# Self attention on one core: token-wise softmax sums folded into the output gates, masked rows on the scalar engine, joins on the vector engine

## The chip, the cores and the metric

The kernel runs on one core of a Trainium2 chip. The engines that matter here are TensorE (PE, with its weight loads listed apart as PEld), VectorE (DVE), ScalarE (ACT) and GpSimd (POOL); each works through its own instructions in program order and waits on semaphores for the others. The metric is the device time of one execution in microseconds (us), as the median of repeated runs.

## The reference, cut to what matters

The program is four layers over x of shape (4, 512, 256): two cross attentions, a routed feed-forward layer, and at the end a self attention with expert gates. The change touches the last one alone:

```python
B, T, D = (4, 512, 256)
H, DH, E, SEL = (8, 64, 5, 2)
q = (x @ Wq).reshape(b, t, h, dh).transpose(0, 2, 1, 3)
k = (x @ Wk).reshape(b, t, h, dh).transpose(0, 2, 1, 3)
gl_v = (x @ Ws).reshape(b, t, h, e)
wv = _topk_mask(gl_v, SEL) * jax.nn.sigmoid(gl_v)
xv = jnp.einsum('btd,edk->btek', x, Wv)
v = jnp.einsum('bthe,btek->bhtk', wv, xv)
scores = jnp.einsum('bhid,bhjd->bhij', q * scale, k)
probs = jax.nn.softmax(scores, axis=-1)
attn = jnp.einsum('bhij,bhjd->bihd', probs, v)
gl_o = (x @ Wd).reshape(b, t, h, e)
mask_o = _topk_mask(gl_o, SEL)
out = jnp.einsum('bthe,bthk,ekd->btd', mask_o, attn, Wo)
```

So a head's attention rows are divided by their softmax sum, copied into five expert columns under a 0/1 mask, summed over the heads, and multiplied with Wo.

## The kernel before

The self layer (names `self_...`) works in 16 steps: 4 batches by 4 pairs of heads (`NP`). A step s handles two heads of one batch, with 512 queries and 4 tiles of 128 keys.

`self_plan` writes one list of items by hand; every engine walks through that same list and takes the items that are its own, so the list is the order on each engine. The items of a step are:

- `K`, `q`: projections for step s+2, six matmuls on PE; ACT copies the high part (`KH`, `QH`), DVE subtracts the low part (`KL`, `QL`). `max`: eight products for step s+1, whose row maxima DVE takes (`part`); from them DVE makes `negtop`, PE turns it (`shift`), ACT copies it (`NM`).
- `S` (scores of one key tile, PE), then the exponential (ACT, `probs`), then `AV` (PE, into `outT`). `evac` copies `outT` to `OT` on ACT. `vmix` builds the values of the next step on DVE: nine products and sums per step (`v_part`, `VN`).
- `add`: sums the exponentials over pairs of key tiles, tiles 0 and 1 on POOL (`acc_pool`), 2 and 3 on DVE (`acc_dve`).
- `sum`: PE sums these over the keys with a matrix of ones, into one bank of [128 x 512] that holds each sum 64 times. ACT takes its logarithm (`lnsum`) and `exp(-...)` of that (`guess`), DVE makes a Newton step (`guess`, `norm`: `newt`) and scales `OT`. `back`: PE turns `OT` into token rows, ACT copies them (`natural`).
- `mix`, on POOL: per tile of 128 tokens `masked` = rows times gates, for 5 experts and 2 heads; `joined` = the two heads added; `mixed` += `joined`. In the last step DVE does three of its four tiles.
- once per batch: loading and normalising x, `turn`, `gate` and `masks` (the ranking of gates, DVE), and at the end `mixT` and `out`.

`K`, `q`, `max`, `shift`, `sum`, `back`, `turn`, `gate`, `mixT` and `out` go through a ring of three PSUM banks; a unit's matmuls wait until the bank of the third unit before has been read. The waits that the change touches are these:

```python
elif kind == "back":                 # PE
    s = item[1]
    pe.wait_ge(normed, s + 1)
...
elif kind == "mix":                  # POOL
    pool.wait_ge(*freed(("back", s)))
    pool.wait_ge(mix_steps, mix_before[s])
```

Of the kernel before, what the change touches and what calls it, by code (L numbers as in the profile page):

```python
# [6 lines left out]
P = 128  # L7
D = 256
NQ = 512
QT = NQ // P  # L10
DH = 64
# [834 lines left out]
def self_plan(B, NP, KT):  # L846

    steps, parts = B * NP, KT // 2
    front, between, mid, tail, late = ([[] for _ in range(steps * parts)] for _ in range(5))
# [4 lines left out]
    for s in range(steps):  # L854
        b, p = divmod(s, NP)
        if s + 1 < steps:
            maxima = [("max", s + 1, qt, h) for qt in range(QT) for h in range(2)]
            put(front, s, 0, *maxima[0:2])
            put(between, s, 0, maxima[2])
            put(mid, s, 0, maxima[3])  # L860
            put(front, s, 1, maxima[4])
            put(between, s, 1, maxima[5])
            put(mid, s, 1, *maxima[6:8])
# [5 lines left out]
        if s + 2 < steps:  # L869
            put(tail, s, 1, ("q", s + 2))  # L870
        if s + 1 < steps:
            put(tail, s, 1, ("shift", s + 1))
        if s:
            put(tail, s, 1, ("back", s - 1))
            put(late, s, 1, ("mix", s - 1))
        if s + 1 < steps:
            for e in range(EXPERTS):
                put(late, s, int(e > 1), ("vmix", s + 1, e))
        more = b + 1 < B
        if p == 0 and more:  # L880
            put(front, s, 0, ("load", b + 1))
        if p == 1:
            if more:
                for ch in range(2):
                    put(tail, s, 1, ("turn", b + 1, "x", ch, 0))
        if p == 2:
            if b:
                put(tail, s, 0, *[("mixT", b - 1, t) for t in range(QT)])
                put(tail, s, 1, *[("out", b - 1, t) for t in range(QT)])
                put(late, s, 1, ("store", b - 1))  # L890
            if more:
                put(tail, s, 0, *[("gate", b + 1, t) for t in range(QT)])
                put(late, s, 0, ("masks", b + 1))
        if p == 3 and b < B:
            put(front, s, 0, ("xload", b))

    for b in range(1, B):
        items, first = norm_items(False, b, KT), (b - 1) * NP * parts
        for k, item in enumerate(items):
            late[first + k * 3 // len(items)].append(item)  # L900
# [5 lines left out]
    plan += [("gate", 0, t) for t in range(QT)] + [("shift", 0), ("masks", 0)]  # L906
    plan += [("K", 1), ("q", 1), ("wsplit", 2), ("wsplit", 3)] + [("vmix", 0, e) for e in range(EXPERTS)]
    for n in range(steps * parts):
        s, d = divmod(n, parts)
        plan += front[n] + [("S", s, 2 * d), *between[n], ("S", s, 2 * d + 1)] + mid[n]  # L910
        plan += [("AV", *divmod(s * KT + 2 * d - 2 + i, KT)) for i in range(2)] if n else []
        plan += [("evac", s - 1)] if d == 0 and s else []
        plan += tail[n] + [("add", s, 2 * d + i) for i in range(2)] + late[n]
    last = steps - 1
    plan += [("AV", last, KT - 2), ("AV", last, KT - 1), ("evac", last), ("sum", last), ("norm", last), ("back", last)]
    plan += [("mix", last)] + [("mixT", B - 1, t) for t in range(QT)] + [("out", B - 1, t) for t in range(QT)]
    plan += [("store", B - 1)]
    for item in [i for i in plan if i[0] == "sum"]:
        behind = plan.index(item) + 1
        units = 0  # L920
        while plan[behind][0] != "norm" and units < BANKS - 1:
            units += plan[behind][0] in SELF_RING
            behind += 1
        plan.insert(behind, ("guess", item[1]))
# [3 lines left out]
def self_layer(nc, name, x_in, x_out, weights, B, NP, KT):  # L928
# [12 lines left out]
    POOL_LAST = (0,)  # L941
# [17 lines left out]
    for s in range(steps):  # L959
        mix_before.append(mix_before[-1] + (len(POOL_LAST) if s == steps - 1 else QT) * (3 if s % NP else 2))  # L960

    ctx = ExitStack()
    with ctx:
# [15 lines left out]
        lnsum, guess, newt = sb("lnsum", [P, NQ]), sb("guess", [P, NQ]), sb("newt", [P, NQ])  # L979
# [4 lines left out]
        masked, joined = sb("masked", [P, QT, EXPERTS, 2, DH]), sb("joined", [P, QT, EXPERTS, DH])  # L984
# [27 lines left out]
        ln_done, guessed, newt_steps, normed = sem("ln_done"), sem("guessed"), sem("newt_steps"), sem("normed")  # L1012
        gate_exp, gate_steps, v_steps = sem("gate_exp"), sem("gate_steps"), sem("v_steps")
        mix_steps, last_mix_steps = sem("mix_steps"), sem("last_mix_steps")
# [13 lines left out]

        def mix(eng, ops, s, tiles, done, base):

            b, p = divmod(s, NP)
            n = len(tiles)
            by = mixed[b % 2][:, :, 0:NV].rearrange("p t (e k) -> p t e k", e=EXPERTS)
            gates = rank[b % 2][:, :, HEADS + 2 * p:HEADS + 2 * p + 2, :].rearrange("p t h e -> p t e h")
            for t in tiles:
# [764 lines left out]
```

## Time and profile before

| | before |
|---|---|
| median of the runs | 2789.59 us |
| the profiled execution, its own time | 2793.12 us |
| its span, first to last instruction | 2791.2 us |
| PE busy | 2370.3 us (85%) |
| DVE busy | 1906.8 us (68%) |
| ACT busy | 1071.1 us (38%) |
| POOL busy | 1071.1 us (38%) |
| TensorE's mean granted clock | 0.927 of full speed |

The busy time of an engine is the union of its instructions' times; an engine that waits for a semaphore is not busy. The granted clock is the share of full speed (2.4 GHz) that the chip gave TensorE; it has two levels, 1.0 and 0.5 (1.2 GHz). All four layers are in these numbers; the self layer is the last 625 us of the span (from 2166 us on).

### The profile page before, as it was taken

To read this page: it belongs to the slowest core of one execution; us is meant where nothing else is said; L and a number is where in the kernel's file an instruction comes from. 1 tells how busy PE (TensorE), PEld (TensorE's weight loads), DVE (VectorE), ACT (ScalarE), POOL (GpSimd) and SP (SyncE) were. 2 spreads that over 40 slices of the span, in tenths; PEclk is the share of its full clock that TensorE was granted. 3 is DMA by queue.
4 is the path that set the end of the run, shared out by engine and by line. 5 is a ranking of instruction groups with operands and counts; after the bars stand their busy time and mean duration, and the time that the engine had idled before them with its cause. 6 is when DMAs were issued, how large, how long until landed. Compare 5 with 4: busy or idle time off the path is not lost. (4 is left out here: it accounts for less than half of the span.)

```text
span 2791.2 us, 34947 instructions
## 1 busy us (share of the span) xinstructions
PE 2370.3 (85%) x12992; PEld 1462.6 (52%) x12992; DVE 1906.8 (68%) x3187; ACT 1071.1 (38%) x1484; POOL 1071.1 (38%) x636
## 2 busy tenths in 40 slices
PE   5999999999999697999999999999998566565756
PEld 3556556655655575655565565556554433332433
DVE  6997898898786676566556655664663567667575
ACT  4555455445453101444434444443443222212222
POOL 3421221222221001655455545454664125444265
PEclk9999999999999787999999999999999678777788
DMA  3000000000000214000000000000000100000000
GB/s 108 12 1 23 16 1 24 16 1 1 16 1 1 61 45 126 13 1 1 23 16 1 1 23 16 1 1 16 1 1 1 56 8 1 0 23 1 15 1 23
DMA packets 62626, 48.54 MB, mean 17 GB/s; under 512 B 12226, under 2 KB 61954, under 8 KB 62466
## 3 DMA queue, kind: packets, MB, share of 16 engines
q1 hardware_dynamic: 62468, 46.40, 5.5%
q8 instruction: 103, 1.69, 0.3%
q14 instruction: 55, 0.45, 0.1%
HBM read 38.01 MB, written 8.39 MB: 17 GB/s over the span
## 5 line engine op out<-in xcount | busy, mean ns | idle before, releaser
L436 POOL TENSOR_TENSOR cross_acc_pool<-cross_acc_pool,cross_probs 128x1024 f32<-128x1024 f32 x192 | 464.3, 2418 | 167.3 <-ACT cross_probs L517 153.2
L422 POOL TENSOR_TENSOR latent_KR<-latent_rot 128x256 f32<-128x256 f32 x128 | 175.9, 1374 | 608.7 <-DVE latent_rot L628 608.7
L634 DVE TENSOR_REDUCE cross_part<-cross_ring 128x1 f32<-128x512 f32 x512 | 322.4, 682 | 102.0 <-PE cross_ring L771 101.9
L517 ACT ACTIVATE cross_probs<-cross_scores 128x1024 f32<-128x1024 f32 x256 | 256.4, 1025 | 171.8 <-PE cross_scores L803 168.1
L517 ACT ACTIVATE latent_probs<-latent_scores 128x1024 f32<-128x1024 f32 x256 | 247.6, 1019 | 87.2 <-PE latent_scores L799 87.2
L663 DVE TENSOR_TENSOR latent_acc_dve<-latent_acc_dve,latent_probs 128x1024 f32<-128x1024 f32 x192 | 257.9, 1343 | 10.0
L819 PE MATMUL cross_outT<-cross_probs,cross_VN 128*64 128x512 f32 x1024 | 251.7, 613 | 0.0
L819 PE MATMUL latent_outT<-latent_probs,latent_VN 128*64 128x512 f32 x1024 | 247.9, 605 | 0.7 <-DVE latent_probs L649 0.7
L1426 PE MATMUL self_ring<-self_KH,self_QH 64*128 64x512 f32 x128 | 57.0, 546 | 205.6 <-DVE self_part L1302 155.1
L436 POOL TENSOR_TENSOR cross_acc_pool<-cross_probs 128x1024 f32<-128x1024 f32 x32 | 76.2, 2381 | 299.0 <-PE cross_ring L831 263.0
L771 PE MATMUL cross_ring<-cross_KH,cross_QH 64*128 64x512 f32 x512 | 153.1, 475 | 40.4 <-DVE cross_newt L670 23.4
L649 DVE TENSOR_SCALAR latent_probs<-latent_probs 128x1024 f32<-128x1024 f32 x256 | 167.5, 693 | 9.9 <-ACT latent_probs L517 9.8
L1036 POOL TENSOR_TENSOR self_masked<-self_natural,self_rank 128x640 f32<-128x640 f32 x61 | 94.6, 1580 | 185.8 <-ACT self_natural L1221 140.9
L694 PE MATMUL latent_ring<-latent_WH,latent_CTH 128*128 128x256 f32 x512 | 157.9, 308 | 0.0
L694 PEld LDWEIGHTS latent_ring<-latent_WH,latent_CTH 128*128 128x128 f32 x512 | 97.0, 189 | 96.2 <-issue 96.1
L1426 PEld LDWEIGHTS self_ring<-self_KH,self_QH 64*128 64x128 f32 x128 | 23.8, 213 | 235.3 <-DVE self_part L1302 165.4
L495 ACT ACTIVATE latent_VN<-latent_ring 128x256 f32<-128x256 f32 x128 | 49.3, 385 | 249.5 <-PE latent_ring L694 249.5
L694 PE MATMUL latent_ring<-latent_WL,latent_CTH 128*128 128x256 f32 x512 | 144.8, 283 | 0.0
L694 PE MATMUL latent_ring<-latent_WH,latent_CTL 128*128 128x256 f32 x512 | 144.3, 282 | 0.0
L771 PEld LDWEIGHTS cross_ring<-cross_KH,cross_QH 64*128 64x128 f32 x512 | 71.6, 190 | 125.0 <-issue 38.0
L607 DVE SCALAR_TENSOR_TENSOR cross_KL<-cross_ring,cross_bqkv,cross_KH 128x512 fp32r<-128x512 f32 x64 | 48.0, 751 | 127.8 <-ACT cross_KH L487 127.8
L819 PEld LDWEIGHTS cross_outT<-cross_probs,cross_VN 128*64 128x64 f32 x1024 | 63.1, 138 | 118.7 <-issue 97.7
(296 smaller groups left out, 5772.2 us busy)
## 6 DMA issues: line engine op xcount, KB each, us to landing
latent_C<-in_ctx_dram SPq DMA_DIRECT2D x4, 1024.0 KB, 6.5
cross_C<-in_ctx_dram SPq DMA_DIRECT2D x4, 1024.0 KB, 6.6
latent_XN<-in_x_dram SPq DMA_DIRECT2D x4, 512.0 KB, 3.9
latent_WRAW<-in_L_xattn_Wkv_dram SPq DMA_DIRECT2D x16, 128.0 KB, 2.4
latent_X<-in_x_dram SPq DMA_DIRECT2D x4, 512.0 KB, 3.8
x_after<-latent_X SPq DMA_DIRECT2D x4, 512.0 KB, 2.9
experts_raw<-in_L_ffn_expert_w_dram SPq DMA_DIRECT2D x1, 2048.0 KB
experts_XN<-x_after SPq DMA_DIRECT2D x4, 512.0 KB, 4.0
```

Of the source, the lines that this page charges most:

```text
L422: nc.gpsimd.tensor_tensor(KR[:, 2 * t:2 * t + 2, :], rot1s[n % 2][:, :, :], rot2s[n % 2][:, :, :], ALU.add)\
L436: nc.gpsimd.tensor_tensor(acc_pool[:, :, :], first[:, :, :], probs[g % PROBS][:, :, :], ALU.add)\
L495: nc.scalar.activation(VN[s % 2][:, 2 * t:2 * t + 2, :], src[:, :, 128:256], ACT.Copy).then_inc(v_copied, 1)
L517: nc.scalar.activation(probs[g % PROBS][:, :, :], scores[g % 2][:, :, :], ACT.Exp, scale=SCALE)\
L634: nc.vector.reduce_max(part[:, qt, h, i:i + 1], bank[:, :], AX.X).then_inc(taken, 1)
L649: nc.vector.tensor_scalar(tile[:, :, :], tile[:, :, :], exp(CLIP), exp(-CLIP), ALU.min, ALU.max)\
L663: nc.vector.tensor_tensor(acc_dve[:, :, :], first[:, :, :], probs[g % PROBS][:, :, :], ALU.add)\
L694: last = nc.tensor.matmul(out, still, moving, start=i == 0, stop=i == len(passes) - 1)
L771: nc.tensor.matmul(bank[:, :], QH[s % QBUF][HEAD[h], qt * P:(qt + 1) * P], KH[s % 2][HEAD[h], i * 512:(i + 1) * 512], start=True, stop=Tru ...
L819: last = nc.tensor.matmul(outT[HEAD[h], :], V[:, t, at + h * DH:at + (h + 1) * DH], probs[g % PROBS][:, h, :], start=t == 0, stop=t == KT - 1)
L1036: ops.tensor_tensor(masked[:, t, :, :, :], natural[s % 2][:, t, :, :].unsqueeze(1).broadcast_to([P, EXPERTS, 2, DH]), gates[:, t, :, :].un ...
L1426: nc.tensor.matmul(bank[:, :], QH[s % 3][HEAD[h], qt * P:(qt + 1) * P], KH[s % 3][HEAD[h], :], start=True, stop=True).then_inc(full, 1)
```

## The change

The sums are taken token by token: `sum` now makes, for each of 4 token tiles and 2 heads, one column of sums in PSUM, with the accumulated exponentials as the stationary operand and one column of ones as the moving one. DVE takes the reciprocal of the resulting 128x8 (`recip`) and multiplies it into that step's gates (`scaled`). The logarithm, `guess`, the Newton step and the scaling of `OT` are gone; `back` turns the unscaled `OT` and waits for `evac` alone.

`mask` takes the place of POOL's masking: for each token tile, ACT makes 10 copies of 128x64 (5 experts by 2 heads), each with one column of `scaled` as its scale. `mix` is now two additions on DVE over all four tiles (one for the first head pair of a batch), from two buffers of `masked`. POOL keeps its one addition per step.

The plan is written anew with four parts per step in place of two: two `max` units at the head of each part, `AV` of a step ending inside it (`evac` in the same step), `sum` and `shift` at its end, `recip` at the head of the next step, the masks of step s-1 in step s (the last tile in step s+1), and `mix` of step s-2 in step s. The ranking of a batch's gates is cut into pieces (`rank`, `gates`).

```diff
+    for s in range(steps):
...
+            for d in range(parts):
+                put(front, s, d, *maxima[2 * d:2 * d + 2])
+            for d, mixes in ((0, (0, 1, 2)), (3, (3, 4))):
+                put(late if d else before, s, d, *[("vmix", s + 1, e) for e in mixes])
         if s + 2 < steps:
             put(tail, s, 0, ("K", s + 2))
+            put(tail, s, 2, ("q", s + 2))
         if s:
-            put(tail, s, 0, ("sum", s - 1))
-            put(tail, s, 1, ("norm", s - 1))
...
+            front[s * parts].insert(0, ("recip", s - 1))
+            put(tail, s, 1, ("back", s - 1), ("mask", s - 1, 0))
+            put(tail, s, 2, ("mask", s - 1, 1))
+            put(late, s, 3, ("mask", s - 1, 2))
+        if s > 1:
+            put(late, s, 0, ("mask", s - 2, 3))
+        put(late, s, 0, ("add", s, 1))
+        if s > 1:
+            put(late, s, 1, ("mix", s - 2))
+        put(before, s, 2, ("add", s, 3))
...
+        put(tail, s, 3, ("sum", s))
+        if s + 1 < steps:
+            put(tail, s, 3, ("shift", s + 1))
...
+        plan += front[n] + [("S", s, 0), ("S", s, 1)] + before[n] + tail[n] + late[n]
+        plan += front[n + 1] + [("S", s, 2), ("S", s, 3), ("AV", s, 0), ("AV", s, 1)] + before[n + 1] + tail[n + 1] + late[n + 1]
+        plan += front[n + 2] + before[n + 2] + tail[n + 2] + late[n + 2]
+        plan += front[n + 3] + [("AV", s, 2), ("AV", s, 3), ("evac", s)] + before[n + 3] + tail[n + 3] + late[n + 3]
...
+                elif kind == "mask":
+                    _, s, t = item
+                    if t == 0:
+                        act.wait_ge(*freed(("back", s)))
+                        act.wait_ge(scales_made, s + 1)
+                        if s >= 2:
+                            act.wait_ge(mix_steps, mix_before[s - 1])
+                    for e in range(EXPERTS):
+                        for h in range(2):
+                            last = nc.scalar.activation(masked[s % 2][:, t, e, h, :], natural[s % 2][:, t, h, :], ACT.Identity,
+                                                        scale=scaled[s % 2][:, t, h, e:e + 1], bias=0.0)
+                    last.then_inc(rows_masked, 1)
...
-                elif kind == "guess":
...
+                elif kind == "recip":
...
+                    dve.wait_ge(full, unit["sum", s] + 1)
+                    nc.vector.reciprocal(recip[:, :, :], total[:, 0:2 * QT].rearrange("p (t h) -> p t h", h=2))\
+                      .then_inc(free[unit["sum", s] % BANKS], 1)
                     dve.wait_ge(*freed(("sum", s)))
...
+                    nc.vector.tensor_tensor(scaled[s % 2][:, :, :, :], gates,
+                                            recip[:, :, :].unsqueeze(3).broadcast_to([P, QT, 2, EXPERTS]), ALU.mult)\
+                      .then_inc(scales_made, 1)
+                elif kind == "mix":
...
+                    dve.wait_ge(rows_masked, QT * (s + 1))
...
+                    nc.vector.tensor_tensor(by, by if p else masked[s % 2][:, :, :, 1, :], masked[s % 2][:, :, :, 0, :], ALU.add)\
+                      .then_inc(mix_steps, 1)
+                    if p:
+                        dve.wait_ge(mix_steps, mix_before[s] + 1)
+                        nc.vector.tensor_tensor(by, by, masked[s % 2][:, :, :, 1, :], ALU.add).then_inc(mix_steps, 1)
...
-                    for acc in (acc_dve, acc_pool):
+                    for t in range(QT):
                         for h in range(2):
-                            last = nc.tensor.matmul(bank[HEAD[h], :], ones[:, :], acc[:, h, :], start=acc is acc_dve,
-                                                    stop=acc is acc_pool)
+                            at = 2 * t + h
+                            for acc in (acc_dve, acc_pool):
+                                last = nc.tensor.matmul(bank[:, at:at + 1], acc[:, h, t * P:(t + 1) * P], ones[:, 0:1],
+                                                        start=acc is acc_dve, stop=acc is acc_pool)
                     last.then_inc(full, 1)
                 elif kind == "back":
                     s = item[1]
-                    pe.wait_ge(normed, s + 1)
+                    pe.wait_ge(evacuated, s + 1)
```

Three places show what the new plan does to the order. First ACT, in a step without the work of a new batch, from one copy of `NM` to the next. Before:

```order
L1187 ACTIVATE self_NM0<-self_ring1 128x512
L1221 ACTIVATE self_natural0<-self_ring2 128x512
L1200 ACTIVATE self_probs0<-self_scores0 128x1024
L1200 ACTIVATE self_probs1<-self_scores1 128x1024
L1208 ACTIVATE self_OT1<-self_outT 128x512
L1185 ACTIVATE self_KH2<-self_ring1 128x512
L1213 ACTIVATE self_lnsum<-self_ring2 128x512
L1215 ACTIVATE self_guess<-self_lnsum 128x512
L1200 ACTIVATE self_probs2<-self_scores0 128x1024
L1200 ACTIVATE self_probs3<-self_scores1 128x1024
L1182 ACTIVATE self_QH2<-self_ring1 128x512
```

and now, of the same stretch:

```order
L1153 ACTIVATE self_NM0<-self_ring0 128x512
L1189 ACTIVATE self_masked0<-self_natural0,self_scaled0 128x64 x10
L1166 ACTIVATE self_probs0<-self_scores0 128x1024
L1166 ACTIVATE self_probs1<-self_scores1 128x1024
L1151 ACTIVATE self_KH2<-self_ring0 128x512
L1189 ACTIVATE self_masked0<-self_natural0,self_scaled0 128x64 x10
L1166 ACTIVATE self_probs2<-self_scores0 128x1024
L1166 ACTIVATE self_probs3<-self_scores1 128x1024
L1178 ACTIVATE self_natural1<-self_ring0 128x512
L1189 ACTIVATE self_masked1<-self_natural1,self_scaled1 128x64 x10
L1148 ACTIVATE self_QH2<-self_ring0 128x512
L1189 ACTIVATE self_masked1<-self_natural1,self_scaled1 128x64 x10
```

The two rows of `lnsum` and `guess` are gone, and four groups of ten small copies stand between `NM` and the exponentials, between `KH` and the exponentials, and on both sides of `QH`.

Second DVE, around the step's sums. Before, from the first use of the sums to the low part of `q`:

```order
L1358 TENSOR_TENSOR self_newt<-self_ring,self_guess 128x512
L1302 TENSOR_REDUCE self_part<-self_ring 128x1 x2
L1307 TENSOR_SCALAR self_negtop<-self_part 128x512
L1362 SCALAR_TENSOR_TENSOR self_newt<-self_newt,self_guess 128x512
L1366 SCALAR_TENSOR_TENSOR self_OT<-self_OT,self_newt 128x512
L1298 TENSOR_TENSOR self_QL<-self_ring,self_QH 128x512
```

and now, from the first use of the sums to the join:

```order
L1337 RECIPROCAL self_recip<-self_ring 128x8
L1343 TENSOR_TENSOR self_scaled<-self_rank,self_recip 128x40
L1255 TENSOR_REDUCE self_part<-self_ring 128x1 x2
L1309 TENSOR_TENSOR self_VN<-self_gated,self_rank 128x512
L1309 TENSOR_TENSOR self_v_part<-self_gated,self_rank 128x512
L1315 TENSOR_TENSOR self_VN<-self_VN,self_v_part 128x512
L1309 TENSOR_TENSOR self_v_part<-self_gated,self_rank 128x512
L1315 TENSOR_TENSOR self_VN<-self_VN,self_v_part 128x512
L1251 TENSOR_TENSOR self_KL<-self_ring,self_KH 128x512
L1255 TENSOR_REDUCE self_part<-self_ring 128x1 x2
L1356 TENSOR_TENSOR self_mixed<-self_mixed,self_masked 128x4x320
L1360 TENSOR_TENSOR self_mixed<-self_mixed,self_masked 128x4x320
```

Three operations on 128x512 have gone from DVE; two small ones and two additions of 1280 columns have come, the additions between the second and the third pair of maxima.

Third PE, at the step's sums, before:

```order
L1386 MATMUL self_ring<-self_XTH,self_WL 128x512
L1471 MATMUL self_ring<-self_acc_dve,self_ones 64x512 x2
L1471 MATMUL self_ring<-self_acc_pool,self_ones 64x512 x2
L1426 MATMUL self_ring<-self_KH,self_QH 128x512
L1447 MATMUL self_scores<-self_QH,self_KH 128x512 x2
```

and now (of the eight equal pairs of rows of the sums one stands):

```order
L1374 MATMUL self_ring<-self_XTH,self_WL 128x512
L1414 MATMUL self_ring<-self_KH,self_QH 128x512 x2
L1450 MATMUL self_outT<-self_probs,self_VN 64x512 x4
L1461 MATMUL self_ring<-self_ones,self_acc_dve 128x1
L1461 MATMUL self_ring<-self_ones,self_acc_pool 128x1
...
L1420 MATMUL self_ring<-self_ident,self_negtop 128x128 x4
```

Sixteen matmuls of one column stand where four of 512 columns stood, and they moved from behind `K`'s projection to between the step's last `AV` and `shift`.

## Rows read from the trace of the kernel before

**Rows 1.** Busy time by stretch: bounds, length, then PE, PEld, DVE, ACT, POOL, PEclk, DMA

```profile
2244.80:2727.20 482.40, 295.01 (x1314) 162.12 (x1316) 328.45 (x429) 119.04 (x172) 213.96 (x155) 0.79 0.02 7
2665.60:2696.40 30.80, 19.30 (x89) 9.96 (x89) 22.76 (x24) 8.12 (x11) 17.14 (x13) 0.83 0.00 0
2583.40:2632.80 49.40, 32.56 (x149) 20.45 (x149) 29.55 (x49) 12.09 (x21) 17.57 (x13) 0.81 0.07 22
2727.20:2747.50 20.30, 18.72 (x110) 12.10 (x108) 12.24 (x18) 8.56 (x13) 10.79 (x8) 1.00 0.08 27
2747.50:2791.20 43.70, 19.41 (x92) 11.41 (x88) 23.08 (x25) 8.64 (x14) 28.07 (x22) 0.80 0.07 24
```

**Rows 2.** Who waited for whom, self layer: us in total, times, longest

```profile
PE self_ring L1426 <- DVE self_part L1302: 155.1, 20, 15.0
```

**Rows 3.** Groups by line and shape, self layer: busy us, mean ns of one, idle before

```profile
L1337 DVE TENSOR_TENSOR self_VN<-self_VN,self_v_part 128x512 f32<-128x512 f32 x64 | 95.6, 1493 | 2.2
L1036 POOL TENSOR_TENSOR self_masked<-self_natural,self_rank 128x640 f32<-128x640 f32 x61 | 94.6, 1580 | 185.8 <-ACT self_natural L1221 140.9 <-issue 22.9 <-PE self_ring L1403 11.5
L1331 DVE TENSOR_TENSOR self_v_part<-self_gated,self_rank 128x512 f32<-128x512 f32 x64 | 76.4, 1194 | 1.1
L1200 ACT ACTIVATE self_probs<-self_scores 128x1024 f32<-128x1024 f32 x64 | 63.9, 1025 | 49.5 <-PE self_scores L1450 47.2
...
L1221 ACT ACTIVATE self_natural<-self_ring 128x512 f32<-128x512 f32 x16 | 9.5, 593 | 8.8 <-PE self_ring L1478 8.8
```

**Rows 4.** Timeline of one plain step: start us, us, engine, line, operation

```profile
2665.50 0.50 PE L1386 MATMUL self_ring<-self_XTH,self_WH 128*128 128x512 f32 x1
2667.10 1.08 PE L1471 MATMUL self_ring<-self_acc_dve,self_ones 128*64 128x512 f32 x4
2669.19 2.77 POOL L1129 TENSOR_TENSOR self_acc_pool<-self_probs 128x1024 f32<-128x1024 f32 x1 [3.64 <-PE self_ring L1471]
2669.76 2.76 DVE L1337 TENSOR_TENSOR self_VN<-self_VN,self_v_part 128x512 f32<-128x512 f32 x1
2670.43 1.95 ACT L1200 ACTIVATE self_probs<-self_scores 128x1024 f32<-128x1024 f32 x2
...
2679.77 1.05 PE L1432 MATMUL self_ring<-self_ident,self_negtop 128*128 128x128 f32 x8
2681.21 1.22 DVE L1351 TENSOR_TENSOR self_acc_dve<-self_probs 128x1024 f32<-128x1024 f32 x1
2682.03 6.59 POOL L1036 TENSOR_TENSOR self_masked<-self_natural,self_rank 128x640 f32<-128x640 f32 x4 [10.06 <-ACT self_natural L1221]
2685.84 1.65 DVE L1331 TENSOR_TENSOR self_v_part<-self_gated,self_rank 128x512 f32<-128x512 f32 x1
```

**Rows 5.** Timeline of DVE in the layer's first step, where POOL has no mix

```profile
2211.72 0.69 DVE L1337 TENSOR_TENSOR self_VN<-self_VN,self_v_part 128x512 f32<-128x512 f32 x1
2212.45 0.69 DVE L1331 TENSOR_TENSOR self_v_part<-self_gated,self_rank 128x512 f32<-128x512 f32 x1
```

**Rows 6.** Timeline of ACT, first layer: copies scaled by a column of a tile

```profile
30.44 0.78 ACT L466 ACTIVATE latent_staging<-latent_ring,latent_gbc 128x512 f32<-128x512 f32 x1
31.10 0.78 ACT L468 ACTIVATE latent_CTH<-latent_ring,latent_gbc 128x512 fp32r<-128x512 f32 x1
```

**Rows 7.** Timeline of PE in the experts layer: matmuls of eight columns

```profile
978.73 0.25 PE L1728 MATMUL experts_routed<-experts_router_low,experts_XThigh 128*128 128x8 f32 x1
978.84 0.25 PE L1728 MATMUL experts_routed<-experts_router_high,experts_XTlow 128*128 128x8 f32 x1
...
980.18 0.35 PE L1728 MATMUL experts_routed<-experts_router_high,experts_XThigh 128*128 128x8 f32 x1
980.40 0.35 PE L1728 MATMUL experts_routed<-experts_router_low,experts_XThigh 128*128 128x8 f32 x1
```

**Rows 8.** Busy time by stretch around them, columns as in rows 1

```profile
982.00:984.00 2.00, 2.00 (x10) 1.90 (x10) 0.38 (x2) 0.00 (x0) 0.00 (x0) 0.50 0.74 242
```

**Rows 9.** Timeline of PE in the cross layer, at full clock

```profile
1661.66 1.94 PE L819 MATMUL cross_outT<-cross_probs,cross_VN 128*64 128x512 f32 x8
```

More of the change, by code:

```diff
@@ L846, in self_plan @@
 def self_plan(B, NP, KT):
-    steps, parts = B * NP, KT // 2
-    front, between, mid, tail, late = ([[] for _ in range(steps * parts)] for _ in range(5))
+    steps, parts = B * NP, 4
+    front, before, tail, late = ([[] for _ in range(steps * parts)] for _ in range(4))
     def put(where, s, d, *items):
@@ L879, in self_plan @@
-        more = b + 1 < B
+            front[s * parts].insert(0, ("recip", s - 1))
[8 more added lines that the diff above has]
+        put(before, s, 2, ("add", s, 3))
         if p == 0 and more:
             put(front, s, 0, ("load", b + 1))
-        if p == 1:
+        if p == 1 and more:
+            for ch in range(2):
+                put(tail, s, 1 + ch, ("turn", b + 1, "x", ch, 0))
+            put(tail, s, 3, ("gate", b + 1, 0), ("gate", b + 1, 1))
@@ L883, in self_plan @@
+        if p == 2:
             if more:
-                for ch in range(2):
-                    put(tail, s, 1, ("turn", b + 1, "x", ch, 0))
-        if p == 2:
+                put(tail, s, 0, ("gate", b + 1, 2), ("gate", b + 1, 3), ("sigm", b + 1))
+                for j in range(EXPERTS):
+                    put(late, s, 1 + j // 2, ("rank", b + 1, j))
+                put(late, s, 3, ("gates", b + 1))
             if b:
[L888 to L893, printed above, removed]
@@ L905, in self_plan @@
     plan += [("max", 0, qt, h) for qt in range(QT) for h in range(2)]
[L906 to L913, printed above, removed]
-    last = steps - 1
[L915 to L924, printed above, removed]
+    plan += [("gate", 0, t) for t in range(QT)] + [("sigm", 0), ("shift", 0)] + [("rank", 0, j) for j in range(EXPERTS)]
+    plan += [("gates", 0), ("K", 1), ("q", 1), ("wsplit", 2), ("wsplit", 3)] + [("vmix", 0, e) for e in range(EXPERTS)]
+    for s in range(steps):
+        n = s * parts
+        plan += front[n] + [("S", s, 0), ("S", s, 1)] + before[n] + tail[n] + late[n]
+        plan += front[n + 1] + [("S", s, 2), ("S", s, 3), ("AV", s, 0), ("AV", s, 1)] + before[n + 1] + tail[n + 1] + late[n + 1]
+        plan += front[n + 2] + before[n + 2] + tail[n + 2] + late[n + 2]
+        plan += front[n + 3] + [("AV", s, 2), ("AV", s, 3), ("evac", s)] + before[n + 3] + tail[n + 3] + late[n + 3]
+    last = steps - 1
+    plan += [("recip", last), ("back", last), ("mask", last - 1, 3), ("mix", last - 1)]
+    plan += [("mask", last, t) for t in range(QT)] + [("mix", last)]
+    plan += [("mixT", B - 1, t) for t in range(QT)] + [("out", B - 1, t) for t in range(QT)] + [("store", B - 1)]
     return plan
@@ L978, in self_layer @@
         acc_dve, acc_pool = sb("acc_dve", [P, 2, NQ]), sb("acc_pool", [P, 2, NQ])
-        lnsum, guess, newt = sb("lnsum", [P, NQ]), sb("guess", [P, NQ]), sb("newt", [P, NQ])
+        recip, scaled = sb("recip", [P, QT, 2]), [sb(f"scaled{i}", [P, QT, 2, EXPERTS]) for i in range(2)]
         VN = [sb(f"VN{i}", [P, QT, 2, DH]) for i in range(2)]
@@ L1147, in _ @@
                 kind = item[0]
-                if kind in ("turn", "gate", "q", "K", "shift", "sum", "back", "mixT"):
+                if kind in ("turn", "gate", "q", "K", "shift", "back", "mixT"):
                     bank = bank_of(item)
```

156 lines of the change are left out of this document (57 added, 99 removed).

## The prediction

> **What bounds the kernel now.** Only the self layer changes, so the page is read for its place (the last 625 us), and the rest by views of that stretch. First the stretches: between the first and the fourteenth copy of `outT` lie 13 steps in 482.4 us, a step without a new batch's work takes 30.8 us, and in it DVE is busy 22.8, PE 19.3, POOL 17.1, ACT 8.1 us, at a mean granted clock of 0.83 [rows 1]. No engine is full; the waits say who is late: PE's max products wait 155.1 us in all for DVE's maxima [rows 2]. Then the groups: DVE's longest are the nine `vmix` operations of each step, whose additions take 1493 ns on average and whose products 1194 [rows 3]. The timelines say why these are long. In the layer's first step, where POOL has no mix, each takes 0.69 us and they follow each other at 0.73 [rows 5]; beside POOL's `masked` the same product takes 1.65, and an addition that meets POOL's `acc_pool` of 2.77 us takes 2.76 [rows 4]. So DVE is the bound, and a good part of its length is POOL's doing. POOL itself waits for `natural` for 140.9 us [rows 3] and sets no end but this.
>
> **What the change costs and saves in a plain step.**
>
> *DVE.* The eight `vmix` operations take 4 x 1.49 + 4 x 1.19 = 10.7 us on average; without POOL's mix they take 8 x 0.72 = 5.8: 5.0 saved (the first product I leave). Three operations of the same 512 columns go, at the same 0.73: 2.2 saved. The two joins are new: 1.22 us for 1024 columns [rows 4] and 0.69 for 512 [rows 5] make 1.04 ns a column, so 1.49 us for 1280 and 3.0 for two. `recip` and `scaled` (8 and 40 columns) have no row; they lie between nothing and 2 x 0.69, I take 0.5 for both, nearer the small end since they have a tenth of the columns. DVE then needs 22.8 - 5.0 - 2.2 + 3.0 + 0.5 = 19.1 us.
>
> *ACT.* The logarithm and the guess go (two operations of `natural`'s shape, 0.6 each). 40 copies of 64 columns come. Two copies of 512 columns scaled and shifted by columns of a tile start 0.66 us apart [rows 6]; two exponentials of 1024, without such an operand, take 1.95 [rows 4], one of them 1.025 [rows 3], so they start 0.93 apart; `natural` shows 0.593 for 512 [rows 3], so a column costs (1.025 - 0.593) / 512 = 0.84 ns. Less the missing columns this leaves 0.29 us from the one and 0.12 from the other; without any overlap it would be 0.40 (0.78 less 448 columns). I take 0.25, nearer the row with such operands: 2.5 us for the ten copies of a tile, 10 a step, bounds 1.2 to 4.0 a tile. ACT then needs 8.1 - 1.2 + 10.0 = 16.9 us. The Trainium skill ("ScalarE: Activation LUTs", What ACT_TABLE_LOAD costs) has a price that no row here has alone, one column operand: 186 ns, 0.833 ns a column and 93 for the operand, of which 93 overlap, an estimate of 0.24 us a copy; the sum would be 0.3 us a step lower by it.
>
> *PE.* At full clock the step's 19.3 busy us are about 19.3 x 0.83 = 16.0. The sums took about 2.0 (two groups of 1.08 that overlap [rows 4]). Sixteen fp32 matmuls of one column come; the four of before show as eight records, so these are 32 pairs of load and matmul with 128 stationary columns. Nearest are the matmuls of eight columns in the experts layer, 0.11 us apart at first and 0.21 apart later [rows 7], when the clock is at its lower level of 1.2 GHz (0.50 [rows 8]): 3.5 us or 6.8. PE needs 16.0 - 2.0 + 3.5 = 17.5 us at full clock. [...]
>
> *POOL* keeps its addition of 2.8 us and the small power for a new batch, which no longer stands behind a mix. The DMA issues on SP wait for the same units as before and have a step or more of room: nothing.
>
> **The path.** Three engines now need 19.1, 17.5 and 16.9 us; their order sets the rest. From one step's last `AV` on, each link waits for the one before: sums 3.5, `shift` 1.0 [rows 4], `NM` 0.6, ten masks 2.5 (they stand before the exponentials on ACT, and the scores pass under them), two exponentials 1.95, `KH` 0.6, ten masks 2.5, two exponentials 1.95, `natural` 0.6 (its bank is the one that `q` takes), `q` 1.6 (from 2665.50 to 2667.10 [rows 4]), a max pair 0.5, two `AV` tiles 1.9 [rows 9]. That is 19.2 us. The new waits on DVE lie close beside it: `recip` waits for the sums, with the maxima and `vmix` behind it; the joins wait for the masks of the last tile, with two maxima, the addition and `QL` behind them, and `sum` behind those. By the same links DVE comes to the joins about half a us before the masks are done, and to `recip` about 0.8 us after the sums. A chain of 19.2 and an engine of 19.1 that wait for each other cannot both run without slip: I take 20.
>
> *The clock* comes on top. With PE busy 18.7 of 20.3 us the grant was 1.00; in the plain step, with gaps of some us, 0.83 [rows 1]. Now PE would be busy 17.5 of 20, but 3.5 of that are one-column matmuls, and in the experts layer a stretch of eight-column ones, PE busy throughout, did not bring the clock back [rows 8]. If the sums fall into the low level they cost 3.3 more, if all of PE's links do, 8.5 (their own length) more; at best nothing. I take 2, near the stretch of 1.00, since that is the row with PE as full. **22 us a step**.
>
> **The sum.** Before, 13 steps were 13 x 30.8 = 400 and the work for new batches 82 us more. In the step of 49.4 us that work is 18.6 us of time, of which 6.8 is DVE's and 13.3 x 0.81 = 10.8 PE's [rows 1]; with DVE and PE both full it cannot hide, so 11 in 18.6: 48 of the 82. 13 x 22 + 48 = 334, 148 less than 482. The first step gains one step's worth, 9. The step of 20.3 us becomes one of 22, 2 lost. The tail of 43.7 us [rows 1] loses POOL's and DVE's last mixes but gets five tiles of masks (12.5) and a join (3.0) in a row: I take 5 lost, bounds 4 gained and 12 lost. In all -150 against the profiled execution's own 2793.1: 2643, and the median of the runs lies 3.5 lower: **2640 us**.
>
> **Rivals.**
> 1. *The masks are dear.* ACT has three groups of them on the chain. At 0.35 us a copy the chain grows by 3.0: 25 us a step, tail 5 more, some 2690; at 0.40 near 2715. For it: the scaled rows are the longest of their shape [rows 6]; against it, they overlap by 0.12 us there.
> 2. *The clock drops at every step's sums.* Then the sums take 6.8 and `shift` 2: 25.5 a step, about 2695. For it [rows 8]; against it the stretch of 1.00.
> 3. *The clock stays low all step: slower.* One-column matmuls once a step might keep PE at 1.2 GHz. PE then needs 35 us plus some 2.4 of waits, and the batches' work 95: 13 x 37.4 + 95 = 581, with first step and tail about 2915. It decides from a mean grant of about 0.6 down: there a step takes 17.5 / 0.6 + 2.4 = 31.6 us, which with some 70 for the batches makes up the 482. Against it: before, with PE idle for 11.5 of 30.8 us, the grant was still 0.83 [rows 1].
> 4. *Less in the way.* Masks at 0.17 and no clock lost: DVE's 19.1 binds, 19.3 a step, batches 42: 2590.
> 5. *The change doesn't do what it says*: `vmix` stays long without POOL's mix, because of its operands. DVE 24, step 25, 2690. [Rows 5], the same instruction at 0.69, speak against it.
>
> **How the numbers follow.** 0.50 for the forecast (its own range 2620 to 2666, steps of 20.5 to 24), 0.12 for rival 4, 0.15 each for 1 and 2, 0.04 each for 3 and 5. The range 2585 to 2715 leaves out rival 3, the far ends of 1, 2 and 4, some 0.17 in all. A measurement here tells 2% from no change, 56 us: all cases but rival 3 and the tails of 1 and 2 lie below 2734. Faster 0.87, same 0.09, slower 0.04.
>
> **What would show it.** Right: `vmix` at 0.69 to 0.72 us but for those under POOL's one addition; plain steps of 20 to 24 us; 128x64 copies 0.2 to 0.3 apart; one-column pairs at 0.11; PE's wait for the maxima all but gone; a grant above 0.85. Wrong: masks at 0.35 or more, a grant near 0.7 with pairs at 0.21, or DVE idle before the joins and `recip` for more than a us each, which would mean that the order and not the work sets the step.

## The result, and the profile after

The changed kernel takes 2665.17 us (median; 2665.16 to 2666.2), the kernel before 2789.59: a ratio of 0.9559, 95% interval 0.9532 to 0.9587, so 4.4% faster. 2640 was predicted, within 2585 to 2715. One of the three runs of the kernel before took 5590 us, and the ratio is taken from the other two. The profiled execution has a span of 2663.4 us and its own time 2665.16, 128.0 less than that of before, where 150 less were forecast.

Busy time by stretch of the kernel after, columns as in [rows 1]: first the 13 steps from the first copy of `outT` to the fourteenth, then two plain steps, the second, third and fourth step of a batch, and what lies behind the sixteenth copy:

```profile
2223.74:2580.22 356.48, 319.34 (x1634) 218.38 (x1634) 259.75 (x440) 220.79 (x646) 34.52 (x15) 0.84 0.03 10
2538.30:2559.99 21.69, 21.26 (x114) 14.48 (x114) 17.27 (x26) 16.23 (x50) 2.61 (x1) 0.84 0.00 1
2559.99:2580.22 20.23, 19.55 (x115) 12.95 (x114) 17.16 (x26) 16.23 (x50) 2.41 (x1) 0.92 0.01 1
2444.19:2475.30 31.11, 26.03 (x121) 16.87 (x122) 22.35 (x36) 17.45 (x52) 2.40 (x1) 0.78 0.00 1
2475.30:2509.55 34.25, 29.27 (x149) 20.32 (x150) 20.00 (x38) 20.28 (x58) 2.55 (x1) 0.85 0.00 1
2509.55:2538.30 28.75, 26.89 (x146) 19.73 (x146) 21.57 (x35) 16.26 (x49) 2.40 (x1) 0.88 0.12 37
2629.56:2663.40 33.84, 13.42 (x51) 11.13 (x51) 8.07 (x10) 17.51 (x67) 0.00 (x0) 0.60 0.05 15
```

Four steps of the 13 count as plain: the first step of the second, third and fourth batch (21.95, 21.94, 21.69 us) and the second step of the last batch (20.23). 22 were predicted, and 30.8 were taken before. PE is now busy in all of a plain step but 0.4 to 1.4 us. The other nine, with a new batch's work, take 26.1 to 34.3. The groups that answer to [rows 3] (self layer, by line and shape: busy us, mean ns of one, idle before):

```profile
L1189 ACT ACTIVATE self_masked<-self_natural,self_scaled 128x64 f32<-128x64 f32 x640 | 159.5, 343 | 0.5
L1315 DVE TENSOR_TENSOR self_VN<-self_VN,self_v_part 128x512 f32<-128x512 f32 x64 | 48.6, 759 | 2.2
L1309 DVE TENSOR_TENSOR self_v_part<-self_gated,self_rank 128x512 f32<-128x512 f32 x64 | 44.2, 690 | 1.7
L1360 DVE TENSOR_TENSOR self_mixed<-self_mixed,self_masked 128x1280 f32<-128x1280 f32 x12 | 17.9, 1492 | 0.4
L1337 DVE RECIPROCAL self_recip<-self_ring 128x8 f32<-128x8 f32 x16 | 3.3, 206 | 17.9 <-PE self_ring L1461 17.8
```

`vmix` fell from 1194 and 1493 ns to 690 and 759. In the plain step of before that [rows 1] and [rows 4] show (2665.60 to 2696.40), these eight operations took more than the layer's means, 7.3 + 5.3 = 12.6 us:

```profile
L1337 DVE TENSOR_TENSOR self_VN<-self_VN,self_v_part 128x512 f32<-128x512 f32 x4 | 7.3, 1822 | 0.1
L1331 DVE TENSOR_TENSOR self_v_part<-self_gated,self_rank 128x512 f32<-128x512 f32 x4 | 5.3, 1333 | 0.1
```

In a plain step now they take 5.5. The waits that answer to [rows 2], in the 13 steps:

```profile
DVE self_XTL L1245 <- ACT self_XTH L1130: 19.4, 6, 5.9
...
PE self_ring L1374 <- DVE self_XTL L1245: 9.7, 3, 3.2
...
PE self_ring L1414 <- ACT self_mixedT L1194: 7.9, 4, 2.4
PE self_ring L1414 <- DVE self_recip L1337: 6.7, 3, 3.5
...
PE self_ring L1414 <- DVE self_part L1255: 2.7, 3, 1.0
```

Before, PE waited for the maxima in the same 13 steps for

```profile
PE self_ring L1426 <- DVE self_part L1302: 144.7, 16, 15.0
```

and now for 2.7 us. What PE waits for now belongs to new batches: turned rows (`XTL`), `mixedT`, and a `recip` that comes late.

The terms of the sum, each by the profiled executions (plain work is 13 times the mean of the plain steps, 21.45 us after; the batches' work is what the 13 steps take beyond that):

| stretch | before | predicted | after |
|---|---|---|---|
| to the first copy of `outT` | 2244.8 | -9 | -21.0 |
| 13 steps | 482.4 | 334 (-148) | 356.5 (-125.9) |
| of these plain work, 13 times a plain step | 400 | 286 | 279 |
| of these the new batches' work | 82 | 48 | 78 |
| fourteenth to fifteenth copy | 20.3 | +2 | 24.4 (+4.1) |
| tail behind the fifteenth copy | 43.7 | +5 | 58.8 (+15.1) |

`evac` now stands in its own step and no longer in the next one, which moves some 11 us from the first line to the last; their sum is -5.9 where -4 was forecast. The plain step was a little shorter than forecast. Nearly all that is missing lies in the batches' work: 78 us and not 48. The experiments ask where that comes from, whether POOL's mix was the cause, and what sets a plain step.

### The profile page after: what moved, and what is told of

It reads as the page before. It is cut to its first block and busy times, and to the rows that moved or that the text cites. A ratio compares the mean times of both kernels' runs of the same rounds, so it can differ in the third digit from the quotient of the medians.

```text
span 2663.4 us, 36143 instructions
## 1 busy us (share of the span) xinstructions
PE 2396.2 (90%) x13376; PEld 1526.1 (57%) x13376; DVE 1830.3 (69%) x3190; ACT 1203.5 (45%) x2092; POOL 857.8 (32%) x469
## 5 line engine op out<-in xcount | busy, mean ns | idle before, releaser
L1189 ACT ACTIVATE self_masked<-self_natural,self_scaled 128x64 f32<-128x64 f32 x640 | 159.5, 343 | 0.5
L1106 POOL TENSOR_TENSOR self_acc_pool<-self_probs 128x1024 f32<-128x1024 f32 x16 | 39.7, 2481 | 361.4 <-ACT self_probs L1166 361.4
L819 PEld LDWEIGHTS latent_outT<-latent_probs,latent_VN 128*64 128x64 f32 x1024 | 62.1, 136 | 108.2 <-issue 106.2
## 6 DMA issues: line engine op xcount, KB each, us to landing
latent_WRAW<-in_L_xattn_Wkv_dram SPq DMA_DIRECT2D x16, 128.0 KB, 2.4
```

Source lines behind the costliest of these rows:

```text
L819: last = nc.tensor.matmul(outT[HEAD[h], :], V[:, t, at + h * DH:at + (h + 1) * DH], probs[g % PROBS][:, h, :], start=t == 0, stop=t == KT - 1)
L1189: last = nc.scalar.activation(masked[s % 2][:, t, e, h, :], natural[s % 2][:, t, h, :], ACT.Identity, scale=scaled[s % 2][:, t, h, e:e + 1 ...
```

## The experiments

Intervals are of the ratio to the kernel before on the same chip. Differences in us are of medians; the runs come from several chips, on which the kernel before took 2788.3 to 2792.0 us. The steps' lengths are distances between copies of `outT` in the profiled run.

**1. Copies ahead of the masks** (e2_copies_first). In the changed kernel ScalarE's copies of turned rows and of `mixedT` stand behind ten masks each.

```diff
-            put(tail, s, 1, ("back", s - 1), ("mask", s - 1, 0))
-            put(tail, s, 2, ("mask", s - 1, 1))
+            put(tail, s, 1, ("back", s - 1))
...
+        if s:                                  # behind the puts of turn and mixT
+            put(tail, s, 1, ("mask", s - 1, 0))
+            put(tail, s, 2, ("mask", s - 1, 1))
```

> The changed kernel with one thing moved: on ScalarE the copies of the turned rows (XTH) and of mixedT, which stand behind ten masks, go ahead of them; PE's order is unchanged. Theory A (the new batch's work is dear because its copies queue behind the masks: PE waits 3.2 us for XTL in the second step of a batch and 2.4 and 1.5 us for mixedT in the third, and the clock falls after these waits): the second steps go from 31.1 to 26 to 28 us, the third from 34.3 to 30 to 32, in all 12 to 25 us less than 2665. Theory B (PE and DVE are full with the batch's own work, some 12 us each per batch, and the waits only show where it lands): less than 5 us gained.

Measured: 2644.0 us, 0.9473 (0.9457 to 0.9489). The second steps of a batch went to 24.1, 28.7 and 28.9 (from 29.8, 31.1, 31.1), the third ones to 27.6, 27.8 and 29.0 (from 26.1, 34.2, 34.3), the 13 steps to this (by stretch):

```profile
2227.63:2563.61 335.98, 308.57 (x1634) 213.52 (x1634) 256.79 (x440) 219.31 (x647) 34.95 (x15) 0.86 0.03 10
```

Theory A by the total, 21 us less; of the steps, the last two second ones stayed above its 26 to 28 and the last two third ones fell below its 30 to 32. The plain steps stayed at 21.5 on average, so the batches' work fell from 78 to 57 us. How the wait ran in the changed kernel is read from the timeline of such a step:

```profile
2460.66 0.47 PEld L1391 LDWEIGHTS self_ring<-self_ident,self_XN 128*128 128x128 f32 x4
...
2461.59 2.50 ACT L1189 ACTIVATE self_masked<-self_natural,self_scaled 128x64 f32<-128x64 f32 x10
...
2464.00 0.58 ACT L1130 ACTIVATE self_XTH<-self_ring 128x512 fp32r<-128x512 f32 x1
2464.61 0.69 DVE L1245 TENSOR_TENSOR self_XTL<-self_ring,self_XTH 128x512 fp32r<-128x512 f32 x1 [5.88 <-ACT self_XTH L1130]
...
2465.36 0.79 PE L1374 MATMUL self_ring<-self_XTH,self_WH 128*128 128x512 f32 x1 [3.24 <-DVE self_XTL L1245]
...
2471.64 3.61 PE L1450 MATMUL self_outT<-self_probs,self_VN 128*64 128x512 f32 x8
```

PE turns the rows at 2460.7, ScalarE copies them only when ten masks are done, DVE and PE wait for that, and after it PE works at its lower level for much of the time: the eight `AV` take 3.61 us, not 1.94 [rows 9].

**2. Sums ahead of gate and out** (e3_sums_first).

```diff
+        put(tail, s, 3, ("sum", s))           # ahead of gate and out
+        if s + 1 < steps:
+            put(tail, s, 3, ("shift", s + 1))
+        outs = p == 2 and b
+        if outs:
+            put(tail, s, 3, ("vmix", s + 1, 3), ("vmix", s + 1, 4), ("recip", s))
```

> The changed kernel with the sums, shift and (where out follows) the last vmix pairs and recip ahead of gate and out in the second and third step of a batch, so that NM comes 2 to 5 us earlier there. Theory A (ScalarE's wait of 9.2 us for NM behind 5.4 us of out, and PE's wait of 1.6 us for recip behind the gates' reciprocal, lengthen the fourth step): 6 to 14 us less than 2665, the fourth steps from 28.8 to 25 to 27. Theory B (PE is the bound there, and the same matmuls in another order take as long): within 3 us.

Measured: 2672.46 us, 0.9578 (0.9562 to 0.9594), 7 us more by the medians, not told apart from the changed kernel. A is wrong, and B's 3 us were missed too: the third steps with `out` lost 1.4 and 0.9 us, but the fourth ones after them grew from 28.7 to 33.2 and 30.8. The order puts scores and maxima behind `out`, and nothing was won by the earlier `NM`. What ScalarE's wait for `NM` costs by itself is not shown by this.

**3. Masks ahead of NM** (e7_mask_ahead).

```diff
-            put(late, s, 3, ("mask", s - 1, 2))
+        if s:
+            put(tail, s, 3, ("mask", s - 1, 2))   # ahead of sum and shift
```

> The changed kernel with the third tile's ten masks ahead of NM on ScalarE, where it idles 4.8 us a step, in place of between NM and the exponentials. Theory A (the masks are on the step's chain, as the prediction says): 1 to 2.5 us a step less, 15 to 40 us in all. Theory B (PE's scores, at the low clock there, end at the same time as these masks, so PE and not ScalarE sets that place): within 8 us of 2665.

Measured: 2667.17 us, 0.9554 (0.9538 to 0.957). Every one of the 15 distances is within 0.06 us of the changed kernel's. B: these ten masks, 2.5 us, lie beside PE's scores and cost nothing.

**4. POOL's work put back** (e5_pool_beside).

```diff
+                    for i in range(8):            # POOL, behind its one addition
+                        pool.wait_ge(spare_steps, 1 + max(0, 8 * s + i - 3))
+                        nc.gpsimd.tensor_tensor(spared[:, i % 4, :], spare[:, :], spare[:, :], ALU.mult).then_inc(spare_steps, 1)
```

> The changed kernel plus eight products of 128x640 on POOL per step, on spare tiles that nobody reads or waits for: as much POOL work beside VectorE as the kernel before had. Theory A (POOL's work beside it is what made vmix long and VectorE the bound): vmix products and sums go from 0.69 and 0.76 us to 1.1 to 1.5 on average, 45 to 90 us more than 2665. Theory B (vmix gets longer, but VectorE has 4 us of idle time in a plain step that takes it): up to 15 us more. Theory C (vmix was long for another reason): vmix stays at 0.7, no change.

Measured: 2714.92 us, 0.9726 (0.971 to 0.9742), 50 us more, from work that nobody waits for. The size is A's, the place was another: in the last two plain steps (24.0 us each, from 21.7 and 20.2) VectorE's groups read

```profile
L1261 DVE TENSOR_REDUCE self_part<-self_ring 128x1 f32<-128x512 f32 x16 | 10.4, 680 | 0.0
L1315 DVE TENSOR_TENSOR self_v_part<-self_gated,self_rank 128x512 f32<-128x512 f32 x8 | 7.6, 953 | 0.2
L1321 DVE TENSOR_TENSOR self_VN<-self_VN,self_v_part 128x512 f32<-128x512 f32 x8 | 5.5, 692 | 0.3
L1366 DVE TENSOR_TENSOR self_mixed<-self_mixed,self_masked 128x1280 f32<-128x1280 f32 x2 | 4.9, 2426 | 0.1
...
L1335 DVE TENSOR_TENSOR self_acc_dve<-self_probs 128x1024 f32<-128x1024 f32 x2 | 4.6, 2282 | 0.0
L1257 DVE TENSOR_TENSOR self_QL<-self_ring,self_QH 128x512 fp32r<-128x512 f32 x3 | 2.0, 677 | 0.0
```

Whatever stands beside POOL's work gets long: the joins 2.43 in place of 1.49, `acc_dve` 2.28 in place of 1.22, some of the products. The maxima and the low parts, which read PSUM, keep their 0.68. In the 13 steps of this trace no engine waits for POOL's additions, so the extra work did not cost by making these late.

**5. The kernel before with POOL idle** (e8_before_pool_idle).

```diff
-                ops.tensor_tensor(masked[:, t, :, :, :], ...
+                ops.tensor_tensor(masked[:, t, :, :, 0:k], ...     # k is 1 on POOL, so for the additions
```

> The kernel before with POOL's mix cut to one column of 64 in each row (its masked rows are left out but for that, so the output is another); everything else, the logarithm and the Newton step too, as before. Theory A (POOL's mix beside VectorE is the larger part of what the change takes away): vmix at 0.7 to 0.8 us, plain steps from 30.8 to 24 to 26, 60 to 95 us less than 2790. Theory B (the change's order is the larger part: where the sums, shift and masks stand): vmix gets short but VectorE then waits, plain steps of 27 to 30, 10 to 45 us less. Theory C (the mix alone explains it): 110 to 130 less, as the change.

Measured: 2700.47 us, 0.9683 (0.9667 to 0.9699), 88 us less than before: 3.2 of the change's 4.4%, some 70%. Its plain steps:

```profile
2570.72:2595.26 24.54, 17.98 (x89) 9.70 (x90) 17.83 (x24) 8.11 (x12) 8.04 (x13) 0.92 0.00 1
2595.26:2621.48 26.22, 19.66 (x89) 10.31 (x89) 17.84 (x24) 8.12 (x11) 8.05 (x13) 0.82 0.00 0
```

VectorE fell from 22.76 to 17.84, by 4.9 where the prediction's term was 5.0, with one `VN` addition a step still at 2.77 beside POOL's `acc_pool`. The other 30% belong to the rest of the change, the smaller work of VectorE and the new order together; no run separates them.

**6. Half of the sums** (e6_half_sums).

```diff
-                            for acc in (acc_dve, acc_pool):
-                                last = nc.tensor.matmul(bank[:, at:at + 1], acc[:, h, t * P:(t + 1) * P], ones[:, 0:1], ...
+                            last = nc.tensor.matmul(bank[:, at:at + 1], acc_dve[:, h, t * P:(t + 1) * P], ones[:, 0:1],
+                                                    start=True, stop=True)
```

> The changed kernel with half of the sums left out: the 16 load-and-matmul pairs with acc_pool are gone, so the divisors hold only the tiles that VectorE adds up and the output is another. Theory A (PE, with the clock that it is granted, sets a plain step now): 1.75 us at the full clock to 3.5 at the low one per step, 28 to 56 us less than 2665 in all, plain steps of 18.5 to 20. Theory B (VectorE's 17.2 us with its waits, or the order, set it): less than 10 us.

Measured: 2644.64 us, 0.9487 (0.9471 to 0.9502), 20.5 us less; less than A asked, more than B. Of the four plain steps one went from 21.69 to 18.51 at a grant of 1.00, with VectorE busy 18.20 of it; the next only from 20.23 to 19.93, and the other two from 21.95 and 21.94 to 21.86 and 21.79, with VectorE busy 21.4 and 21.3 of them, for there a `VN` addition of 2.8 us meets POOL's addition again. So PE set the first of these steps, and VectorE stands close behind: at some 18.2 us there, and at the whole step where its `vmix` meets POOL.

**7. Wide products for the sums** (e12_wide_sums).

```diff
-                            ...   # 32 pairs with one column
+                    for i in range(15):
+                        last = nc.tensor.matmul(bank[:, :], KH[s % 3][:, 0:P], KH[s % 3][:, :], start=i == 0, stop=i == 14)
```

> The changed kernel with the 32 pairs of each step's sums replaced by 15 products of KH with itself, 512 columns each and 0.23 us apart, so the same 3.5 us of PE without one-column matmuls; the divisors are then no softmax sums and the output is another. Theory A (the one-column matmuls are why the clock falls to its lower level behind every step's sums): the grant of the plain steps goes from 0.84 and 0.92 to 0.97 or more, plain steps of 18.5 to 19.5 us, 25 to 45 us less than 2665. Theory B (PE's waits around shift, NM and the maxima are why): grant and steps as they are, within 8 us of 2665.

Measured: 2642.92 us, 0.9476 (0.9462 to 0.9491), 22 us less. The two plain steps:

```profile
2523.68:2542.53 18.85, 18.10 (x96) 11.23 (x95) 17.13 (x26) 15.82 (x50) 2.60 (x1) 1.00 0.00 1
2542.53:2561.43 18.90, 18.17 (x96) 11.33 (x95) 17.13 (x26) 15.82 (x50) 2.60 (x1) 1.00 0.00 0
```

A for the clock and the steps (grant 1.00, 18.9 us; the other two plain steps 19.2 and 20.1, also at 1.00), while the total stayed 3 us short of its 25. With as much PE time and the same waits, only the matmuls of the sums changed, but in three ways: 15 products in place of 32 pairs, 512 columns in place of one, and the type of `KH` (fp32r) in place of fp32. Which of the three the clock follows is not separated. In the changed kernel the fall is seen among the sums themselves or just behind them (timeline of PE):

```profile
2539.50 0.36 PE L1461 MATMUL self_ring<-self_ones,self_acc_dve 128*128 128x1 f32 x2
2539.72 0.36 PE L1461 MATMUL self_ring<-self_ones,self_acc_pool 128*128 128x1 f32 x2
...
2540.73 0.57 PE L1461 MATMUL self_ring<-self_ones,self_acc_dve 128*128 128x1 f32 x2
2541.16 0.56 PE L1461 MATMUL self_ring<-self_ones,self_acc_pool 128*128 128x1 f32 x2
2541.58 2.05 PE L1420 MATMUL self_ring<-self_ident,self_negtop 128*128 128x128 f32 x8
```

Two pairs start 0.22 us apart, then 0.43, and `shift` and the next step's first scores are paid at the low level. By the clock as the traces record it, TensorE went to the lower level between 3.1 us before and 1.6 us behind the end of the sums in all 16 steps of the changed kernel, and in none of the 16 with wide products.

**8. One accumulator** (e9_one_total), on top of experiment 1: `total` adds `acc_pool` to `acc_dve`, and 16 pairs are left.

```diff
+        put(late, s, 2, ("total", s))
...
+                    nc.vector.tensor_tensor(acc_dve[:, :, :], acc_dve[:, :, :], acc_pool[:, :, :], ALU.add).then_inc(totalled, 1)
```

> The kernel with the copies of turned rows and mixedT first, and one more change: VectorE adds acc_pool to acc_dve (1.22 us) behind QL, and PE sums one accumulator, 16 pairs in place of 32 (1.75 us less at the full clock). Theory A (PE sets the plain step and VectorE has room): 0.7 to 1.5 us a step less, 12 to 25 us below 2644. Theory B (the addition stands ahead of the last maxima, shift waits for it, and VectorE sets the step): no gain, up to 15 us more.

Measured: 2632.06 us, 0.9438 (0.9422 to 0.9454), 12 below experiment 1, the small end of A.

**9. The gates behind recip** (e10_gates_late), on top of experiment 1.

```diff
-                put(late, s, 3, ("gates", b + 1))
...
+            if more:                               # in the fourth step
+                put(front, s, 0, ("rank", b + 1, EXPERTS - 1), ("gates", b + 1))
```

> The kernel with the copies of turned rows and mixedT first, and one more change: the last rank piece and the gates' step (3.3 us of VectorE with a reciprocal of 1.15) go behind recip and the first two maxima of a batch's fourth step. Theory A (PE waits 7.1 us in the layer for recip, up to 4.2 at a time, and these waits are time): 5 to 12 us below 2644, the fourth steps from 28.7 to 25.5 to 27.5. Theory B (what goes behind recip delays vmix and KL as much): within 4 us.

Measured: 2640.27 us, 0.947 (0.9454 to 0.9485): 3.7 less by the medians, not told apart from 0.9473. PE's waits for `recip` fell from 7.1 to 1.9 us, and the first fourth step from 27.0 to 25.4, but the other two grew from 28.3 and 28.7 to 30.2 and 29.4. B.

**10. The three together** (e11_joined).

> The three edits that each gained, together: copies of turned rows and mixedT ahead of the masks, one accumulator summed, the gates' step behind recip. Theory A (each took away another wait): 2628, that is 12 and 4 us below the 2644 of the first alone. Theory B (with one accumulator VectorE sets the step, and what goes behind recip delays it): 2632 to 2638.

Measured: 2635.63 us (2630.78 to 2639.19), 0.9452 (0.944 to 0.9465). A is wrong, and the size is B's; it is no better than experiment 8 alone.

**11 and 12. Sums in two stages** (e13_wide_then_few on top of experiment 1, e14_wide_one on top of 1 and 8): wide sums as before the change, a ScalarE copy, and `cols`, which turns them token by token in eight pairs.

```diff
+                    nc.scalar.activation(sumT[:, :], bank[:, :], ACT.Copy).then_inc(taken, 1)
...
+                elif kind == "cols":
+                    for t in range(QT):
+                        last = nc.tensor.matmul(bank[:, 2 * t:2 * t + 2], sumT[:, t * P:(t + 1) * P], sel[:, :], start=True, stop=True)
```

> The kernel with the copies first, its sums in two stages: four products of 512 columns as in the kernel before (2.0 us of PE), one ScalarE copy of them (0.6 us), and behind shift four products of the copy with two columns, eight pairs of 0.11 us. In all 2.9 us of PE in place of 3.5, and 8 narrow pairs in place of 32. Theory A (the many narrow pairs are what takes the clock down, as the run with wide products says): grant of plain steps 0.95 or more, plain steps of 18.8 to 20 us, 15 to 30 us below 2644. Theory B (the copy between the two stages makes PE wait and the clock falls for that): within 8 us of 2644.

> The same with one accumulator: VectorE adds acc_pool to acc_dve, so the first stage is two products in place of four (1.0 us of PE less), VectorE has 1.22 us more a step. Theory A (PE still sets the step): 8 to 15 us below the kernel of two stages. Theory B (at full clock VectorE, 17.2 us and its waits, sets it): the same or up to 10 us more.

Measured: 2624.55 us, 0.9407 (0.9392 to 0.9423), the best version here, and 2627.21 us, 0.9422 (0.9406 to 0.9438). The gain is A's (19.5 below experiment 1), the plain steps are not: the grant rose to 0.90 to 0.99, but the steps stayed at 20.5 to 22.1 (20.2 to 22.0 in experiment 1), the last two with VectorE busy 19.9 and 19.5. In the 13 steps the gain is 16 us, and it lies in those with a new batch's work. One `VN` addition a step now meets POOL's addition again (timeline of VectorE, first of the two runs):

```profile
2510.59 2.76 DVE L1327 TENSOR_TENSOR self_VN<-self_VN,self_v_part 128x512 f32<-128x512 f32 x1
```

With one accumulator the grant is 1.00 in the last two plain steps and VectorE is busy 20.01 of 20.45 us: B of the last.

## Why the prediction held, step by step

- **VectorE's saving by POOL's absence: right in its cause, and in its size in part by luck.** 4.9 us by experiment 5 against 5.0; products at 0.69. But the 5.0 took the layer's means (10.7 us) for a plain step whose eight operations took 12.6, and set all eight at 0.72, though it expected one beside POOL's addition, which experiment 5 has at 2.77: two slips that cancel. In the changed kernel they take 5.5, so 7.1 us went, because the new order also keeps `vmix` clear of that addition in nearly all steps. This is most of why VectorE needs 17.2 and not 19.1 us. The three operations gone and the joins (1.49 each) were as forecast, `recip` and `scaled` 0.41 against 0.5. That `vmix` is long for another reason (rival 5) falls by experiments 4 and 5.
- **The masks: right.** Ten take 2.50 us, 0.25 each; a row shows 343 ns, so they overlap and start (2.50 - 0.343) / 9 = 0.24 us apart. The Trainium skill's price ("ScalarE: Activation LUTs", What ACT_TABLE_LOAD costs) made an estimate of 0.24 a copy; the trace agrees. Rival 1 fell; it had counted three groups of masks on the chain, where the path lists two.
- **PE's work: right.** 21.26 x 0.84 = 17.9 us at full clock, against 17.5. The pairs stood 0.11 apart, and 0.21 at the low level. The Trainium skill ("TensorE: Matmul & The Clock Gate", LDWEIGHTS (loading the stationary operand)) gives a load's time as its columns over 1.2, an estimate of 107 ns for 128, and names no clock; the pairs at full clock agree with that, those at the low level do not.
- **The path of 19.2 with VectorE's 19.1 and a slip: wrong in kind, right in size by luck.** 20 of the 22 us were to be a chain through masks and exponentials. Experiment 3 moves ten masks off it and nothing changes; PE is busy 21.26 of 21.69 us, and with wide products or half of the sums that step is 18.5 to 18.9. PE at its granted clock is the bound there, with some 17.9 us of work at full clock, and VectorE, 17 to 18, the next; experiment 6 shows how close behind it stands.
- **The clock's 2 us: right in size.** By experiment 7 it is 2.8 and 1.3 us in the two plain steps. Its cause is rival 2's, the one-column sums. But the clock fell only near their end (most pairs still stood 0.11 apart) and for a part of each step, so that rival's 25.5 us did not come (its own terms, 3.3 and 1.0 on 20, make 24.3); a grant above 0.85 came in one of the two.
- **The batches' work: the step that failed.** "11 in 18.6: 48 of the 82" took it to be limited by VectorE's and PE's own work. It stayed at 78 (82 before). The change puts ten masks ahead of the copies that a new batch needs, and PE and VectorE wait behind them; with the copies first (experiment 1) the 13 steps take 336.0 and this work 57, so 20.5 of the 30 us missing were this wait with the clock that it lost. The term had put no wait between engines into this work. Where the other 9 come from stays open: experiments 2 and 9 moved two other waits and gained nothing that can be told.
- **The start and the tail** traded 11 us by the place of `evac`; their sum was off by 2, as was the step between the fourteenth and the fifteenth copy (4.1 lost where 2 were forecast). The profiled execution lies 22 us above its forecast: 30 more in the batches' work, 7 less in the plain steps, and the rest nearly cancels. 2665 is at the upper end of the forecast's own 2620 to 2666.

## What to carry to other kernels

A slow elementwise engine can be costly without ever being late: look whether another engine's operations are longer beside it than alone, and price its removal by the row that stands alone. When a step's work is moved to an idle engine in groups, look what else goes through that engine once in a while; a group of 2.5 us ahead of a copy that two engines wait for cost a sixth of what this change gained. Narrow matmuls can cost more than their own time, by the clock behind them: 15 wide products in the place of 32 one-column pairs, with the same PE time, were worth 22 us, and sums in wide products with few narrow ones behind them gained 19.5, with some 0.6 us of PE a step less as well.

## What the runs showed of the hardware

- VectorE beside POOL: an addition or product of two tiles in SBUF takes up to four times as long (0.69 to 2.76 us beside `acc_pool`, the joins 1.49 to 2.43); maxima and low parts, which read PSUM, keep 0.68 (experiment 4). The Trainium skill ("VectorE: DVE Perf Modes", Two Vector instructions with no wait between them) says that the second of two SBUF inputs goes through a read interface shared with GpSimd; the additions, products and joins agree with that. It does not cover `negtop`, which reads one tile of SBUF and took 0.43 us alone and up to 1.27 in experiment 4.
- Stretches of 32 one-column fp32 pairs, PE busy throughout, ended at the lower of the clock's two levels or were followed by it at once (grant 0.84 and 0.92 in two plain steps); the same 3.5 us of 512-column products (fp32r) left the grant of these steps at 1.00 (experiment 7).
- 64-column ScalarE copies with a column operand show 343 ns each and start 240 ns apart.
